# Attention and FFN in one kernel: the row maxima's high and low parts made by ScalarE's copy and by a product with minus the identity inside PV, and their transfers issued ahead of the regrouping

## What is computed

```python
qkv = xn @ w_qkv.T + b_qkv                     # 16 heads of 16
att = q @ k.T / sqrt(16) + bias[head, i - j]   # a position bias, from cos and sin features
att = softmax(where(causal, att, -inf))
x + (att @ v) @ w_proj.T + b_proj + ffn(xn)    # ffn: fp8-quantised product with a 256x256 matrix
```

## Time and profile before

| | |
|---|---|
| median of three runs | 897.9 us (895.06 to 902.52) |
| the profiled execution | 896.9 us |
| its span | 895.1 us |
| mean granted TensorE clock | 0.928 |
| TensorE matmul, VectorE, ScalarE, GpSimd busy | 87%, 79%, 65%, 59% |
| DMA | mean 119 GB/s |

### The profile page before, as it was taken

The page is one execution under the profiler, slowest core; times in us unless marked ns, Lnnn a source line. Parts: engine busy times, 40 slices in busy tenths (PEclk is TensorE's granted clock), DMA queues, the critical chain, the costliest instruction groups (busy, mean ns, idle before and its releaser), DMA issues.

```text
span 895.1 us, 22882 instructions
## 1 busy us (share of the span) xinstructions
PE 780.2 (87%) x6121; PEld 497.1 (56%) x6121; DVE 709.3 (79%) x2523; ACT 582.3 (65%) x1194; POOL 525.4 (59%) x522
## 2 busy tenths in 40 slices
PE   6689889899888889988888999889899988889883
PEld 4456546565555556555555655565565556556442
DVE  4778888879788888978888898878889787878702
ACT  4257767676676667667676767767676676776650
POOL 6425656665656655565675567566566656647450
PEclk8769999999999999989999999999999899999885
DMA  5826575556556655755765575566656556665202
GB/s 155 174 64 111 107 151 111 134 105 154 95 118 153 121 125 96 162 89 116 153 122 128 108 156 100 122 125 131 139 101 149 95 125 122 131 122 113 65 15 78
DMA packets 55549, 106.08 MB, mean 119 GB/s; under 512 B 10464, under 2 KB 30432, under 8 KB 55520
## 3 DMA queue, kind: packets, MB, share of 16 engines
q1 hardware_dynamic: 55048, 105.19, 56.8%
q10 hardware_dynamic: 472, 0.54, 0.2%
HBM read 18.68 MB, written 8.91 MB: 31 GB/s over the span
## 4 chain that ended last, share of the span: by engine, by line
PE 42%; SPq 16%; DVE 14%; issue 12%; DMA 9%; ACT 5%; DVEq 1%; ACTq 0%; POOL 0%; POOLq 0%
PE misc_a L645 10%; SPq L323 7%; PE misc_a L534 6%; SPq L371 5%; PE scoreT_a L623 4%; DMA stacks<-neg_max_T 4%; PE scoreT_b L623 4%; PE misc_b L534 4%; SPq L370 3%; DVE score_c L956 3%; PE misc_b L645 3%; DVE row_max L956 3%; PE score_a L600 3%; PE score_c L600 3%; ACT out_T L857 2%
## 5 line engine op out<-in xcount | busy, mean ns | idle before, releaser
L1173 POOL TENSOR_SCALAR_AFFINE_SELECT probs<-probs 128x512 f32<-128x512 f32 x256 | 165.3, 658 | 320.4 <-ACT probs L878 319.1
L956 DVE CUSTOM_DVE_ANT_0 score_b<-score_b,causal_mask_q 128x384 f32<-128x384 f32 (+3 forms) x321 | 161.5, 519 | 104.0 <-PE score_b L600 103.4
L956 DVE CUSTOM_DVE_ANT_0 score_a<-score_a,causal_mask_q 128x512 f32<-128x512 f32 x319 | 171.1, 552 | 21.4 <-PE score_a L600 18.1
L956 DVE CUSTOM_DVE_ANT_0 score_c<-score_c,causal_mask_q 128x256 f32<-128x256 f32 (+3 forms) x384 | 169.1, 467 | 2.4 <-PE score_c L600 2.3
L878 ACT ACTIVATE probs<-scoreT_a 128x512 f32<-128x512 f32 (+1 forms) x256 | 140.4, 548 | 38.9 <-PE scoreT_a L623 30.0
L878 ACT ACTIVATE probs<-scoreT_b 128x384 f32<-128x384 f32 (+1 forms) x256 | 131.4, 513 | 48.9 <-PE scoreT_b L623 39.9
L623 PE MATMUL scoreT_a<-stacks 64*128 64x512 f32 (+3 forms) x320 | 116.9, 378 | 44.7 <-DMA stacks<-neg_max_T 35.9
L956 DVE DVE_READ_ACCUMULATOR2_ANT row_max<- 128x1 f32 x1024 | 141.4, 138 | 0.0
L878 ACT ACTIVATE probs<-scoreT_c 128x384 f32<-128x384 f32 (+1 forms) x256 | 132.4, 517 | 11.5 <-PE scoreT_c L626 10.4
L645 PE MATMUL misc_a<-probs,v_ones 128*32 128x128 f32 (+3 forms) x1536 | 126.7, 473 | 0.4 <-POOL probs L1173 0.4
L623 PE MATMUL scoreT_b<-stacks 64*128 64x384 f32 (+3 forms) x320 | 123.0, 404 | 2.1 <-ACT probs L878 1.3
(11 more groups left out here) (235 smaller groups left out, 1979.3 us busy)
## 6 DMA issues: line engine op xcount, KB each, us to landing
stacks<-qk_parts SPq DMA_DIRECT2D x128, 512.0 KB, 8.2
x_ring<-in_L_attn_x SPq DMA_DIRECT2D x16, 512.0 KB, 3.6
attn<-out_T SPq DMA_DIRECT2D x64, 128.0 KB, 3.8
xn<-recips SPq DMA_DIRECT2D x31, 256.0 KB
out<-x_ring SPq DMA_DIRECT2D x15, 512.0 KB, 3.0
stacks<-neg_max_T SPq DMA_DIRECT2D x128, 4.0 KB
low_features<-neg_max_T SPq DMA_DIRECT2D x124, 4.0 KB
low_features<-probs SPq DMA_DIRECT2D x8, 128.0 KB, 5.0
```

The lines of the kernel that those rows point to most:

```text
L956: last = V.tensor_tensor_reduce(bank, bank, CMQ[:, T - w:T], 1.0, LEAST, ALU.add, ALU.max, MX[:, g % 2, h, qt:qt + 1])
L1173: last = GP.affine_select(out=d, in_=d, compare_op=ALU.is_ge, fill=0.0, base=0, pattern=[[0, HU], [1, P]], channel_multiplier=-1)
```

## The change

- `MX` becomes [128, 2, 72]: for each head, four places for the high parts and four for the whole maxima, and in a second half the high parts again at places shifted by four, all else zero. `chunk_max` writes the whole maxima into it.
- ScalarE's new `max_hi` writes the rounded high parts into both halves in one activation (128 x 32), at slot 2 (in the first unit slot 4), ahead of that slot's exponential. VectorE's `max_hi` and `max_lo` go.
- `job_MT` is two accumulated fp32 products in place of a transpose: 32 columns of `MX` with the identity and 32 with minus the identity (`NID`, made by GpSimd at the start). The sum is the high part and, whole minus high, the low part. It is called inside `pv`, after the products of j = 0.
- ScalarE does `max_T` ahead of `out_T`. In SyncE's queue `load_max` stands ahead of `regroup` in units 1 to 3, not in unit 0.
- Slots on VectorE: `T_lo` of the second half from (0, 2) to (0, 0), `result` from (3, 7) to (3, 6), `quant_magic` from (2, 2), (2, 3), (2, 5) to (2, 0), (2, 1), (2, 2).

```diff
-RESULT_AT = [(3, 1), (3, 7)]
+RESULT_AT = [(3, 1), (3, 6)]
-XL_AT, FIRST_XL_AT = [(3, 10), (0, 2)], [(0, 3), (0, 3)]
+XL_AT, FIRST_XL_AT = [(3, 10), (0, 0)], [(0, 3), (0, 3)]
-MAGIC_AT = [(2, 2), (2, 3), (2, 5)]
+MAGIC_AT = [(2, 0), (2, 1), (2, 2)]
...
+                load_max(b, 2)
                 regroup(b, 0, first)
-                load_max(b, 2)
...
+                load_max(b, 3)
                 regroup(b, 1, first)
-                load_max(b, 3)
...
-                regroup(b, 2, first)
                 if not last:
                     load_max(b + 1, 0)
+                regroup(b, 2, first)
...
-                nc.tensor.transpose(bank[0:HU * 2 * TT, 0:P],
-                                    MXP[:, g % 2, :, :, :].rearrange("p h i t -> p (h i t)").bitcast(F32),
-                                    IDF[:, :]).then_inc(mt_ready, 1)
+                for part, ident in enumerate((IDF, NID)):
+                    last = mm(bank[0:HU * 2 * TT, 0:P], MX[:, g % 2, 32 * part:32 * part + 32], ident[:, :],
+                              start=(part == 0), stop=(part == 1))
+                last.then_inc(mt_ready, 1)
...
+                    if j == 0 and then:
+                        job_MT(*then)
                 last.then_inc(pv_done, 1)
...
+            def max_hi(b, g):
+
+                act.wait_ge(max_done, ROW * b + CHUNKS * (g + 1))
+                whole = MX[:, g % 2, 0:32].rearrange("p (h i t) -> p h i t", i=2, t=TT)[:, :, 1, :]
+                both = MX[:, g % 2, :].rearrange("p (c n) -> p c n", c=2)[:, :, 0:32] \
+                    .rearrange("p c (h i t) -> p c h i t", i=2, t=TT)[:, :, :, 0, :]
+                A(both.bitcast(F32R), whole.unsqueeze(1).broadcast_to([P, 2, HU, TT]), ACT.Copy).then_inc(mh_done, 1)
...
+                        if (g, k) == FIRST_MAX_AT if first and g == 0 else k == MAX_AT:
+                            if not (last and g == 3):
+                                max_hi(*((b, g + 1) if g < 3 else (b + 1, 0)))
                         if k == OUT_AT and not (first and g == 0):
-                            out_T(pb, pg, first and pg == 0)
                             if not (last and g == 3):
                                 max_T(*((b, g + 1) if g < 3 else (b + 1, 0)))
+                            out_T(pb, pg, first and pg == 0)
...
-            def max_hi(b, g):
-
-                dve.wait_ge(max_done, ROW * b + CHUNKS * (g + 1))
-                V.tensor_copy(MXP[:, g % 2, :, 0, :], MX[:, g % 2, :, :]).then_inc(mx_hi, 1)
-
-            def max_lo(b, g):
-
-                dve.wait_ge(mx_hi, 4 * b + g + 1)
-                V.tensor_tensor(MXP[:, g % 2, :, 1, :], MX[:, g % 2, :, :], MXP[:, g % 2, :, 0, :].bitcast(F32),
-                                ALU.subtract).then_inc(mh_done, 1)
...
+            GP.memset(MX[:, :, :], 0.0).then_inc(consts_made, 1)
+            GP.memset(NID[:, :], 0.0).then_inc(ident_steps, 1)
+            pool.wait_ge(ident_steps, 7)
+            GP.affine_select(out=NID[:, :], in_=NID[:, :], compare_op=ALU.not_equal, fill=-1.0, base=0,
+                             pattern=[[-1, P]], channel_multiplier=1).then_inc(ident_steps, 1)
```

More of the change, by code:

```diff
@@ L62 @@
 FIRST_MT_OUT_AT = (0, 6)
+MAX_AT, FIRST_MAX_AT = 2, (0, 4)
 QK_HI_AT, QK_LO_AT = [(0, 6), (0, 9), (1, 6), (1, 9)], [(0, 7), (0, 10), (1, 7), (1, 10)]
@@ L158, in build @@
         Y1 = XB[:, :, :].rearrange("p a n -> p (a n)").rearrange("p (t c) -> p t c", c=C)
-        MX = sb("row_max", [P, 2, HU, TT], F32)
-        MXP = sb("row_max_parts", [P, 2, HU, 2, TT], F32R)
+        MX = sb("row_max", [P, 2, 72], F32)
         MTS = sb("neg_max_T", [HU * 2 * TT, 2, P], F32R)
@@ L174, in build @@
         IDF = sb("ident_f32", [P, P], F32)
+        NID = sb("neg_ident_f32", [P, P], F32)
         CMQ = sb("causal_mask_q", [P, T], BF16)
@@ L247, in build @@
         max_done = sem("chunk_max_done")
-        mx_hi = sem("max_hi_written")
-        mh_done = sem("max_parts_written")
+        mh_done = sem("max_hi_written")
         mt_ready = sem("max_T_in_psum")
@@ L435, in _ @@
             sp.wait_ge(feat_parts, 1)
-            sp.wait_ge(consts_made, 2)
+            sp.wait_ge(consts_made, 3)
             load_low_features(0)
@@ L636, in in_turn, with pv @@
                     streams = [x for x in streams if next(x, streams) is not streams]
-            def pv(b, g, first):
+            def pv(b, g, first, then):
                 if g == 0:
@@ L702, in _ @@
                 in_turn(scores(0, 0, c, n))
+            pe.wait_ge(ident_steps, 8)
             job_MT(0, 0)
@@ L705, in _ @@
                 in_turn(scores(0, 1, c))
-            pe.wait_ge(consts_made, 3)
+            pe.wait_ge(consts_made, 4)
             pe.wait_ge(bp_made, 1)
@@ L725, in body @@
                         if (g, k) == PV_AT[pg] and not (first and g == 0):
-                            pv(pb, pg, first)
-                        if due([FIRST_MT_AT] if first and g == 0 else MT_AT, g, k) and not (last and g == 3):
-                            job_MT(*((b, g + 1) if g < 3 else (b + 1, 0)))
+                            pv(pb, pg, first, None if last and g == 3 else (b, g + 1) if g < 3 else (b + 1, 0))
+                        if first and (g, k) == FIRST_MT_AT:
+                            job_MT(b, 1)
                         if (g, k) == FIRST_T_AT and first:
@@ L751, in _ @@
             body(B - 1, False, True, False)
-            pv(B - 1, 3, False)
+            pv(B - 1, 3, False, None)
             banks = [STB[0], STB[1], SB_[0], SB_[1]]
@@ L841, in _ @@
                 V_evac(0, i)
+            max_hi(0, 0)
             max_T(0, 0)
@@ L956, in chunk_max @@
                     last = V.tensor_tensor_reduce(bank, bank, CMQ[:, T - w:T], 1.0, LEAST, ALU.add, ALU.max,
-                                                  MX[:, g % 2, h, qt:qt + 1])
+                                                  MX[:, g % 2, 8 * h + 4 + qt:8 * h + 5 + qt])
                 last.then_inc(max_done, 1)
-            def max_hi(b, g):
-                dve.wait_ge(max_done, ROW * b + CHUNKS * (g + 1))
-                V.tensor_copy(MXP[:, g % 2, :, 0, :], MX[:, g % 2, :, :]).then_inc(mx_hi, 1)
-            def max_lo(b, g):
-                dve.wait_ge(mx_hi, 4 * b + g + 1)
-                V.tensor_tensor(MXP[:, g % 2, :, 1, :], MX[:, g % 2, :, :], MXP[:, g % 2, :, 0, :].bitcast(F32),
-                                ALU.subtract).then_inc(mh_done, 1)
             def invert(b):
@@ L1053, in _ @@
             V.tensor_tensor(BP[:, :], STB[0][:, 0:C], BP[:, :], ALU.add).then_inc(bp_made, 1)
+            dve.wait_ge(consts_made, 1)
             for n, c in enumerate(FIRST_CHUNKS):
                 chunk_max(0, 0, c, n)
-            max_hi(0, 0)
-            max_lo(0, 0)
             for t in range(TT):
@@ L1075, in body @@
                             chunk_max(nb, ng, k)
-                        if not (last and g == 3):
-                            unit = (b, g + 1) if g < 3 else (b + 1, 0)
-                            start = EARLY if first and g == 0 else 0
-                            if k == start:
-                                max_hi(*unit)
-                            if k == start + 1:
-                                max_lo(*unit)
                         if not last:
```

## The result

The changed kernel takes 822.68 us (median of four runs, 820.63 to 822.75), the one before 897.91 (four runs, 895.06 to 902.52): ratio 0.9152, interval 0.9111 to 0.9193. The profiled execution took 822.72 us, its span 821.0, with a mean granted clock of 0.960. The forecast was 840, with 812 to 875 as its range.

A forecast was written before the change was run, and what follows sets the result against it. TensorE, busy for 87% of the span, was taken as the bound, paid for in its gaps. Terms summed to 49 us over 14 periods plus 9 outside, 58 off 896.9: 839, as a median 840; range 812 to 875.

The forecast's parts named there:

- rival 3: Unit 0's gain comes in full, no new wait at unit 1, product hides: 20 us more, 820; chance 0.11.
- Maxima ahead of the regrouping, +26: Start of unit 2: TensorE's wait for the maxima falls from 2.14 to 0.3 us a period, 26 us gained.
- The clock, +18: After unit 2's wait: the clock drop goes with the wait, 1.3 of 1.5 us a period, 18 us gained.
- Unit 0, +4: 1.28 us ahead of the transpose go, but unit 1's transfers land no sooner: 0.3 us a period, 4 us gained.
- VectorE at the start of unit 1, +11: VectorE catches up during the new wait at unit 1 and TensorE's waits for it go: 0.8 us a period, 11 us.
- quant_magic, -5: Unit 2, new slots: TensorE waits 0.6 us a period at slot 6, 8 us, less 3 back: 5 us lost.
- Rival 2: Unit 2: moved quantising pieces lock behind GpSimd, 0.5 us each for three, 21 us lost, 861; chance 0.12.
- `result` at (3, 6), +6: Unit 3: the bank of xn's transposition comes free one slot sooner, 0.40 us a period, 6 us gained.
- unit 0's own maxima, +3: Start of unit 0: its maxima, landing 0.2 us late once a period, gain from the new order, 3 us.
- rival 4: Product inside PV makes TensorE wait with PV open for a late bank reader: 927 at 1.4 us a unit; chance 0.04.
- The product, -14: Inside PV: two fp32 products in place of one transpose cost 0.25 us each time, 14 us in 14 periods.
- ScalarE's rounding, 0: 64 small activations of 0.26 us cost nothing where ScalarE waits for TensorE; 15 us without that cover.

The follow-up runs named there:

- the filler: Kernel before, with eight added bf16 products on constants where TensorE would wait for unit 2's maxima: 891.8 us, ratio 0.992.
- The slots alone: Kernel before with only `xnT_lo` moved to (0,0), `result` to (3,6), `quant_magic` to (2,0) to (2,2): 873.9 us, ratio 0.973.
- The copy of the small pieces on zeros: Changed kernel with VectorE's small copy and subtraction put back at slots 0 and 1 after the first batch, on zeros, unread: 845.0 us, ratio 0.940.
- the kernel with the order alone: Kernel before with its transpose inside PV, `max_T` ahead of `out_T`, maxima ahead of the regrouping; VectorE's halves and old slots kept: 914.7 us, ratio 1.020.
- three parts: Each on the kernel before: ScalarE's rounding with products behind PV, ratio 0.986; moved slots, 0.973; new order with the transposition inside PV, 1.020.

## Why the prediction was right, and where it was off

The time fell into the range, 17 us below the forecast, on the side of rival 3 (820). The period shrank by 4.9 us where the sum had 3.5. The waits, the clock and VectorE's busy time moved as the signs named in advance said, but for the low features' wait, which stayed at 7.5 us. That the total came within 17 us is in part luck: single terms were off by 18, 11 and 8 us, and they pulled in both directions. Term by term:

**Maxima ahead of the regrouping, +26: right.** The wait at unit 2 is 0.27 us on average over 14 periods, 1.02 at most, where I had kept 0.3. The bound from the stack copies was real: the four issues were stretched to 6.41 us, past the upper end that I had taken for them, and TensorE still waits for them in 8 of the 14 periods. Taken out of the changed kernel, the order costs 67 us and not the 44 of this term and the clock's, because every other gain then ends in the same queue. Put in by itself, with the transposition inside PV, it costs 17. The sum treated it as a term; it is a condition for the others.

**The clock, +18: right in sign, too large as a term.** The granted clock is 1.00 over 14 periods. Before, the period that I read had lost 1.5 us to it; by the mean of 0.96 over all 14 it was some 2 us. By the filler the return in unit 2 is 0.72 us, 10 us over 14 periods, because VectorE takes the rest there. That VectorE's relief let the changed kernel keep more of it is argued, not shown.

**Unit 0, +4: the mechanism right, the size off.** Unit 0's chain sets unit 1's start, as I wrote; the row `low_features` stays (7.5 us, I had said about 15). But "nothing in the change moves it" failed. These are its first score and its queue in the kernel before, ahead of the maxima's issue at 262.66:

```profile
253.83 0.49 PE L623 MATMUL scoreT_a<-stacks 64*128 64x512 f32 x1 [0.16 <-DMA low_features<-neg_max_T]
```

```profile
253.94 1.28 SPq L355 DMA_DIRECT2D stacks<-qk_parts  x2
260.04 0.55 SPq L370 DMA_DIRECT2D attn<-out_T  x1
260.63 1.80 SPq L371 DMA_DIRECT2D denominators<-out_T  x1
```

Before, the denominators' issue took 1.80 us and the maxima's first issue stood 8.83 us behind the unit's first score; after, 0.63 us, and 295.45 stands 8.20 us behind the first score (287.25). Over 13 periods the means are 8.73 and 8.27, and the unit is 0.61 us shorter, the product's cost included. Of the chain that I had read as fixed, 1.2 us was a stretched issue, and `out_T` could come half a microsecond later without being noticed. With `xnT_lo` back at (0, 2) the 0.61 us are gone again, though the issue stays short, since the product then holds PV up and `out_T` starts 0.61 us later.

**VectorE at the start of unit 1, +11: nothing came of it.** TensorE's wait at `score_c` is 7.0 us against 7.2, in the same place, once a period. VectorE did not catch up, since the wait in which it should have is 0.15 to 0.2 us in most periods and not 0.3 or more. The mechanism was right and its condition missing: with the product behind PV, where TensorE waits about 1 us for the low features, `score_c` waits for VectorE only 0.8 us in 3. Unit 1 gained 1.95 us, not 2.4.

**quant_magic, -5: wrong in sign.** This is the step that failed most. I had followed slots by VectorE's 0.7 us each and got 0.6 us of wait for TensorE at slot 6; no such wait is in the trace (2.4 us at `score_a` in all). And I priced the old place by the kernel before, at 3 us. There the third piece lost 7.2 us behind GpSimd's `attn_lo` in all; in the faster kernel it would have lost 15, for its slot then falls under more of that instruction. Measured, the move gains 13.6 us: 18 us off, more than the whole error of the forecast. Rival 2 (these pieces locked at the new place) is refuted: 0.68 or 0.69 us each, but for one of 1135 ns in the first of the 14 periods. Clock, quant_magic and product make 0.72 + 1.11 - 0.20 = 1.63 us for unit 2, which gained 1.66; but the first of these was measured on the kernel before, where all the moved slots together gave unit 2 only 0.29 us, so that the sum meets the gain proves little.

**`result` at (3, 6), +6, and unit 0's own maxima, +3:** the 5.3 us wait for `result` is gone, and unit 3 gained 0.74 us, where these with the product had been 0.4. The slots alone, of which only `result` stands in unit 3, shorten it by 0.35 us, near the 0.40 of the sum. The copy of the small pieces on zeros shows that unit 3 is where the lock hurt: `result` at slot 1, the reader of the product's bank, stands behind the locked subtraction. I had named that bank as the close one in rival 4, and taken no gain from it.

**The product, -14: right.** A pair costs 0.44 us by doubling it, near the 0.47 that PV's rate gave. Net of the transposition it is 0.20, by three timelines: from PV's start to the next score 2.71 us (290.20 to 292.91) inside PV, 2.70 behind it (580.06 to 582.76), 2.51 before, 0.20 a unit and 12 us over 62 units. Nothing of it hides beside PV's columns, the lower bound. In unit 3 the wait for `result` inside PV adds 0.34 us.

**ScalarE's rounding, 0: nothing speaks against it.** 64 activations, median 229 ns, ahead of exponentials whose bank is not yet needed. In unit 3 the weight loads wait for them (14.6 us in 14), with PV's first products still running; of matmuls one waits, for 0.2 us.

**What the terms leave out.** Set side by side as measured over 14 periods (26 for the wait, 10 for the clock, 11 for unit 0 before its product, 2 and 5 for unit 0's maxima and `result`, 15 for quant_magic, less 11 for the product and 5 for its wait in unit 3), they make an estimate of 53 us of the 68 that were gained. Most of the rest lies in unit 3, which gained 0.74 us where 0.35 - 0.20 - 0.34 would have lost 0.2. The small pieces on zeros, which nobody reads, cost 22 us, 1.30 us of each unit 3, and the sum had no term for that. They point at VectorE's relief as the rest; that it is the rest is not shown.

**Rival 4** was given 0.04 on the ground that `xnT_lo` and `result` come sooner themselves. That reason held, and the kernel with the order alone shows what it was worth: without it 914.7 us.

## What to carry to other kernels

When several waits end in one queue, price an edit with the others in and with the others out: here three parts are worth 1.4%, 2.7% and -2.0% alone and 8.5% together, and one piece of the third, the place inside PV, turned out to be worth nothing with all the others in. Also, a gain that only lets an engine arrive sooner at the next transfer shows as a longer wait there. A job put inside an open accumulation needs its bank's last reader and its inputs early; find those readers first, and the engine on which they queue, and ask whether the job has to go there at all. When pieces are moved between slots, follow the old place's full cost (an experiment with only that constant undone is cheap) before taking a small number for it: what a piece loses behind another engine depends on when the two meet, and a faster kernel moves that.

## What the runs showed of the hardware

The issue of a small DMA is no constant. Four of 4 KB took 2.72 us when begun 7.8 us behind the first of two stack copies of 512 KB, and 6.41 us when begun 2.3 us behind it. The denominators' issue took 0.63 us or 2.25; in unit 0 it took 0.63 us when begun 7.5 us behind those copies, 1.80 at 6.7 and 1.39 at 6.8. DMA: Bandwidth & Descriptors in the Trainium skill (Queues, rings and completion order) has descriptors consumed in ring order on each engine, which goes with small transfers that are held up behind the copies.

A VectorE operation on 16 elements a partition took from 0.16 to 2.38 us, by what GpSimd had running, and a quantising piece of 0.69 us took 1.73 to 1.86 us in the same slot of 14 batches, with the old places, while `attn_lo` ran. Two fp32 products with 32 columns of weights and 128 moving took 0.44 us between PV's products, by doubling them, and PV with one pair takes 2.71 us to the next score whether the pair stands inside it or behind: beside PV's column groups they did not run for nothing.

The granted clock, at 0.5 for some microseconds after each gap of about 2.1 us in the kernel before, stays at 1.00 in the 14 periods of the changed kernel, whose largest wait of TensorE is 1.02 us.
